# Selective-scan kernel: tiles of 4 states by 32 channels in place of one state by 128 channels

## What is computed

```
proj = x @ W_in.T;  hs, gate = split(proj);  hs = silu(causal_conv4(hs) + conv_b)
dt_r, Bm, Cm = split(hs @ W_x.T);  dt = softplus(dt_r @ W_dt.T + b_dt);  A = -exp(A_log)
state = exp(dt * A) * state + dt * B_t * u_t        # [128 channels, 16 states], per step
y = sum over states of state * C_t;  y = (y + hs * Dp) * silu(gate);  out = y @ W_out.T
```

## Time and profile before

| | us |
|---|---|
| median of 3 runs (lowest, highest) | 967.57 (965.07, 967.77) |
| profiled execution | 965.7 |
| its span | 963.9 |

### The profile page before, as it was taken

The page is one execution under the profiler, slowest core; times in us unless marked ns, Lnnn a source line. Parts: engine busy times, 40 slices in busy tenths (PEclk is TensorE's granted clock), DMA queues, the critical chain, the costliest instruction groups (busy, mean ns, idle before and its releaser), DMA issues.

```text
span 963.9 us, 8874 instructions
## 1 busy us (share of the span) xinstructions
PE 846.2 (88%) x2178; PEld 363.3 (38%) x2178; DVE 839.9 (87%) x632; ACT 585.7 (61%) x798; POOL 819.0 (85%) x374
## 2 busy tenths in 40 slices
PE   5688989989898899989989898998989889898776
PEld 2233433334443334334343333333443333433322
DVE  2489999888999988998998999999899989889991
ACT  3575765848476583855758486574857657484331
POOL 0598997979989797997989799898989979798990
PEclk9799999989999998989999999999999999899997
DMA  1699688978778798778869788896988779689760
GB/s 46 222 295 305 244 274 285 315 261 281 262 291 303 260 313 293 260 252 288 314 255 318 266 282 258 306 312 253 309 283 280 262 285 325 244 301 302 263 247 3
DMA packets 78051, 258.35 MB, mean 268 GB/s; under 512 B 13104, under 2 KB 15408, under 8 KB 78000
## 3 DMA queue, kind: packets, MB, share of 16 engines
q1 hardware_dynamic: 78000, 257.79, 77.4%
HBM read 254.60 MB, written 3.15 MB: 267 GB/s over the span
## 4 chain that ended last, share of the span: by engine, by line
POOL 51%; DMA 17%; issue 17%; PE 6%; DVE 5%; ACT 3%; SPq 1%; POOLq 1%; DVEq 0%; ACTq 0%
POOL inp L881 31%; POOL state L887 17%; DMA b_all<-bc_dram 14%; DMA c_all<-bc_dram 3%; POOL du L871 3%; DVE ps_x L1031 2%; PE ps_y L546 1%; DVE state L1031 1%; PE ps_w L459 1%; DVE state L1038 1%; ACT ps_x L730 1%; PE ps_x L531 1%; SPq L308 0%; PE ps_w L507 0%; POOL step L873 0%
## 5 line engine op out<-in xcount | busy, mean ns | idle before, releaser
L881 POOL TENSOR_TENSOR inp<-du,b_all 128x1024 f32<-128x1024 f32 x224 | 521.9, 2354 | 4.9 <-DMA b_all<-bc_dram 4.0
L546 PE MATMUL ps_y<-state,packed 128*128 128x512 f32 x1024 | 495.6, 623 | 19.5 <-POOL state L887 19.5
L1031 DVE TENSOR_TENSOR_SCAN ps_x<-ps_x,inp 128x1024 f32<-128x1024 f32 x144 | 329.3, 2287 | 42.5 <-ACT ps_x L730 29.8
L887 POOL TENSOR_TENSOR state<-state,c_all 128x1024 f32<-128x1024 f32 x112 | 262.0, 2351 | 87.0 <-DVE state L1024 49.4
L730 ACT ACTIVATE ps_x<-step,a_neg 128x1024 f32<-128x1024 f32 x224 | 247.1, 1112 | 137.7 <-DVE state L1038 101.0
L546 PEld LDWEIGHTS ps_y<-state,packed 128*128 128x128 f32 x1024 | 194.2, 197 | 267.5 <-issue 213.0
L1038 DVE TENSOR_TENSOR state<-ps_x,c_all 128x1024 f32<-128x1024 f32 x144 | 175.9, 1222 | 4.2 <-issue 0.7
L1031 DVE TENSOR_TENSOR_SCAN state<-ps_x,inp 128x1024 f32<-128x1024 f32 x80 | 179.1, 2272 | 0.0
L531 PE MATMUL ps_x<-u,w_b_wide 128*128 128x512 f32 x128 | 68.0, 656 | 9.4 <-DVE state L1038 9.3
L1024 DVE TENSOR_TENSOR_SCAN state<-decay,ps_x 128x1024 f32<-128x1024 f32 x32 | 73.0, 2281 | 0.5
L459 PE MATMUL ps_w<-xpad,w_conv 128*128 128x512 f32 x128 | 61.6, 605 | 3.3 <-ACT xpad L692 3.3
(11 more groups left out here) (116 smaller groups left out, 676.4 us busy)
## 6 DMA issues: line engine op xcount, KB each, us to landing
c_all<-bc_dram SPq DMA_DIRECT2D x256, 512.0 KB, 6.8
b_all<-bc_dram SPq DMA_DIRECT2D x224, 512.0 KB, 6.0
xt<-in_x_t SPq DMA_DIRECT2D x32, 64.0 KB, 3.3
bc_dram<-bc_rows SPq DMA_DIRECT2D x32, 64.0 KB, 3.2
out<-ofin SPq DMA_DIRECT2D x16, 64.0 KB, 1.6
packed<-in_packed SPq DMA_DIRECT2D x1, 635.0 KB, 4.2
packed<-in_packed SPq DMA_DIRECT2D x1, 129.0 KB, 2.1
w_qkv<-in_w_qkv SPq DMA_DIRECT2D x1, 64.0 KB, 2.2
```

The source lines that it names most:

```text
L546: last = mm(ps_y[:, HALF * half:HALF * (half + 1)], ident, state[n % H_RING][:, HALF * half:HALF * (half + 1)], start=(n == 0), stop=(n == ...
L881: tt(inp[i % IN_RING][:, :], du[b.buf][:, :], b_all[i % B_RING][:, :], ALU.mult).then_inc(pool_inputs, 1)
L887: tt(state[n % H_RING][:, :], state[n % H_RING][:, :], c_all[n % C_RING][:, :], ALU.mult).then_inc(pool_products, 1)
L1031: v.tensor_tensor_scan(held if KIND[n] == "P" else x, x, inp[i % IN_RING][:, :], 0.0, ALU.mult, ALU.add).then_inc(scans, 1)
```

## The change

A tile is now 4 states by 32 channels: tile n = 4m + q holds states 4m to 4m+3 (quad m) of channels 32q to 32q+31 (group q); partition 4i + k is channel i, state k. There are still 16 tiles of [128, 1024] per image, with the same four pieces of work.

- B and C: one load carries the four rows of a quad, repeated 32 times, and serves its 4 tiles: 4 loads of B and 4 of C per image in place of 14 and 16. Rings of 3.
- step and du have one value per channel; each of the 4 groups needs its 32 rows repeated 4 times. SP makes these `step_q` and `du_q` by DMA from SBUF to SBUF (`copy_step`, `copy_du`), 4 and 4 per image, in rings of 6. step and du themselves have one buffer instead of two, so `softplus` and `scan_weight` of the next image wait for the copies of the image before. `copy_step` needs also the first elements of each sequence set to a large step (`stops_set`), which POOL does after du.
- Sums: `sum_quad` replaces `sum_state`. A quad's 4 tiles are summed over the states into the 4 groups of 32 rows of `ps_y`, by matmuls with a stationary tile of 32 columns; it waits for the products of all four tiles.
- KIND has 3 D, 5 P and 8 C in place of 2 D, 5 P and 9 C.
- The softmax's normalisation moves from DVE to ACT: 1 / sum as exp(-ln(sum)), and two scaled copies.
- `mean_square` of the image after next follows its `attn_out`, and all orders are written anew. `prologue` and `finish` are fitted to them.

```diff
-H_RING, C_RING, IN_RING, B_RING, D_RING, X2_RING = 8, 4, 4, 4, 4, 3
+H_RING, C_RING, IN_RING, B_RING, D_RING, X2_RING = 8, 3, 4, 3, 2, 3
+STEP_RING, DU_RING = 6, 6
...
+QUAD, GROUPS = 4, 4
+ROWS = I // GROUPS
...
-KIND = "DCCPDCCCCPPCPPCC"
+KIND = "DPPCCCDCPPCDCCPC"
...
+            def copy_step(j, q):
+
+                o = GROUPS * j.num + q
+                sp.wait_ge(stops_set, j.num + 1)
+                if o >= STEP_RING:
+                    before = o - STEP_RING
+                    all_at_least(sp, *decays_waits(before // GROUPS, tiles_of_group(before % GROUPS)))
+                sp.dma_start(step_q[o % STEP_RING][:, :],
+                             step[ROWS * q:ROWS * (q + 1), :].unsqueeze(1).broadcast_to([ROWS, QUAD, T])
+                             ).then_inc(step_copied[o % STEP_RING], 16)
...
+            def copy_du(j, q):
...
+                sp.dma_start(du_q[o % DU_RING][:, :],
+                             du[ROWS * q:ROWS * (q + 1), :].unsqueeze(1).broadcast_to([ROWS, QUAD, T])
...
+            def load_b(b, m):
...
+                             bc_dram[b.buf][QUAD * m:QUAD * (m + 1), :].unsqueeze(0).broadcast_to([ROWS, QUAD, T])
...
+            def load_c(b, m):
...
+                sp.dma_start(c_all[o % C_RING][:, :],
+                             bc_dram[b.buf][N + QUAD * m:N + QUAD * (m + 1), :].unsqueeze(0
+                                            ).broadcast_to([ROWS, QUAD, T])).then_inc(c_loaded[o % C_RING], 16)
...
+            def sum_quad(b, m):
+
+                all_at_least(pe, *products_waits(b.num, tiles_of_quad(m)))
+                if m == 0:
...
                 for half in range(2):
-                    last = mm(ps_y[:, HALF * half:HALF * (half + 1)], ident,
-                              state[n % H_RING][:, HALF * half:HALF * (half + 1)],
-                              start=(n == 0), stop=(n == N - 1))
+                    for q in range(GROUPS):
+                        last = mm(ps_y[ROWS * q:ROWS * (q + 1), HALF * half:HALF * (half + 1)], w("sum_w"),
+                                  state[(GROUPS * m + q) % H_RING][:, HALF * half:HALF * (half + 1)],
+                                  start=(m == 0), stop=(m == QUAD - 1))
                 last.then_inc(sums, 1)
...
+            def attn_norm(j):
+                act.wait_ge(esc_done, j.num + 1)
+                f(lsum[:, :], esum[:, :], ACT.Ln).then_inc(lsum_done, 1)
+                act.wait_ge(lsum_done, j.num + 1)
+                f(erec[:, :], lsum[:, :], ACT.Exp, scale=-1.0).then_inc(erec_done, 1)
+                act.wait_ge(erec_done, j.num + 1)
+                at_least(act, attn_t_ps, j.num)
+                for k in range(CHUNKS):
+                    last = f(attn[:, k, :], attn_bank(j)[:, POOLED * k:POOLED * (k + 1)], ACT.Copy,
+                             scale=erec[:, k:k + 1])
+                last.then_inc(attn_done, 1)
...
-                at_least(act, du_done, j.num - 1)
-                f(step[j.buf][:, :], ps_w[:, :], ACT.Softplus, bias=w("b_dt")).then_inc(step_done, 1)
+                if j.num > 0:
+                    for q in range(GROUPS):
+                        o = GROUPS * (j.num - 1) + q
+                        act.wait_ge(step_copied[o % STEP_RING], 16 * (o // STEP_RING + 1))
+                f(step[:, :], ps_w[:, :], ACT.Softplus, bias=w("b_dt")).then_inc(step_done, 1)
```

More of the change, by code:

```diff
@@ new lines, in load_b @@
+            def load_b(b, m):
+                if m not in LOADED:
+                    return
+                o = NLB * b.num + LOADED.index(m)
+                sp.wait_ge(bc_stored, 32 * (b.num + 1))
+                if o >= B_RING:
+                    before = o - B_RING
+                    all_at_least(sp, *[(s, v) for s, v in inputs_waits(
+                        before // NLB, tiles_of_quad(LOADED[before % NLB])) if s is pool_inputs])
+                sp.dma_start(b_all[o % B_RING][:, :],
+                             bc_dram[b.buf][QUAD * m:QUAD * (m + 1), :].unsqueeze(0).broadcast_to([ROWS, QUAD, T])
+                             ).then_inc(b_loaded[o % B_RING], 16)
@@ L338, in prologue @@
                 load_x(first + 1)
+                copy_step(first, 0)
                 store_bc(first)
+                copy_du(first, 0)
+                copy_step(first, 1)
+                copy_step(first, 2)
+                copy_du(first, 1)
+                load_b(first, 0)
+                copy_du(first, 2)
+                load_c(first, 0)
                 load_b(first, 1)
+                copy_du(first, 3)
+                copy_step(first, 3)
                 load_b(first, 2)
-                load_b(first, 3)
-                load_b(first, 5)
-                load_c(first, 0)
                 load_c(first, 1)
-                load_c(first, 2)
-                load_b(first, 6)
-                load_c(first, 3)
             def finish(j):
@@ L638, in steps @@
                     attn_out(later)
+                    mean_square(later)
+                sum_quad(b, 3)
             program(pe, prologue, steps, finish)
@@ L780, in prologue @@
                 softmax_exp(first)
+                attn_norm(first)
                 state_decay()
@@ L1066, in prologue @@
                 attn_setup()
-                attn_norm(first)
                 conv_setup()
@@ L1083, in steps @@
                 scan(b, 0)
-                scan(b, 1)
+                if coming:
+                    rms(coming)
                 if done:
                     gated(done)
-                if coming:
-                    rms(coming)
-                product(b, 1)
+                scan(b, 1)
                 scan(b, 2)
-                product(b, 2)
                 scan(b, 3)
@@ L1103, in steps @@
                 scan(b, 8)
[L1104 removed]
                 scan(b, 9)
                 scan(b, 10)
+                if later:
+                    pooling(later)
+                scan_input(b, 11)
+                product(b, 10)
                 scan(b, 11)
+                scan(b, 12)
+                if later:
+                    row_max(later)
+                scan(b, 13)
+                product(b, 12)
                 if done:
                     out_norm(done)
[L1110 to L1117 removed]
+                product(b, 13)
                 scan(b, 14)
[L1119 removed]
                 scan(b, 15)
```

298 lines of the change are left out of this document (146 added, 152 removed).

## The result

The changed kernel takes 1026.6 us (median of 4 runs, 1016.8 to 1033.1) where the kernel before takes 966.3 on the same chip: a ratio of 1.061 [1.058, 1.065]. It is 6% slower; the ratio leaves out the one run of 1033.1 us, which fell in a slower state of the chip. The forecast was 930 us, 4% faster.

The account below looks back on a forecast made before the run. DVE's floor of 51.6 us per image plus waits of 0.2, 0.9, 1.2 and 0.3 gave 54.2 for 56.63; with start +4.5 and end -5, span 927, plus 1.8 and 1.2: 930 us, range 898 to 960.

Parts of the forecast that it names:

- the DMA term: Bunched copies and loads behind decay 12: third transfer lands after 8 us, just in time for POOL's input 1, costing nothing.
- L: Time from issue of copy_step 2 until load_b 0 lands; taken as 8 us, bounds 6 to 18.
- The rival with 8%: Copies bound the round from gated, 43.3 + L; decides from L = 10.9, slower from 13.3; 980 us at 14; chance 8%.
- DVE and POOL: Work per image on these two engines after the change: DVE 51.6 us, POOL 51.1 us.
- Which waits make it up: Waits added to DVE's 51.6 us per image: 0.2 decay 9, 0.9 spread 11, 1.2 closing, 0.3 conv 1 and spread 6.
- the closing term: PE from attn_turn at the low clock through spread 0 to sum_quad 3 ends at 49.5, not 48.3: 1.2 us per image.
- Quad sums: The eight matmuls of a sum_quad on PE run together in 2.1 us, bounds 2.1 to 7.5.
- PE's work: PE's work per image falls from 51 us to about 31.
- DMA share: Share of the time the DMA engines are busy: about 0.45 after the change, from 0.82.
- PE's clock: Two falls per image after idling, before bc_proj and before attn_turn; mean granted clock 0.7 to 0.85 of full.
- POOL's hole: POOL's 4.47 us wait per image ahead of product 0, to be filled by inputs 3 and 4.
- The start: First image waits for copies before its first B: scan 1 at about 47, +4.5 us, bounds +2 to +8.

Follow-up runs that it names:

- spread-source kernel: Changed kernel with channels regrouped (group q holds channels 4i + q), so each SBUF copy reads every fourth partition, not 32 neighbours: 943.5 us, 0.979 of the kernel before.

## Why the prediction was wrong, step by step

**The step that failed** is the DMA term: "I take 8, nearer to the loads, since a copy moves the same 128 rows of 4 KB". It looked at what a copy writes and not at what it reads. Decay 12 of the image shown ended at 514.1, and POOL had B rows at 525.7: L = 11.7 (mean of 15 images 12.0), inside the bounds of 6 to 18, but above the 10.9 from which the prediction let the copies be the bound. In the spread-source kernel decay 12 ended at 523.5 and POOL had B at 531.1: 7.6. The 8 that I took is what the bunch costs when its copies read partitions spread over all 128.

**The rival with 8% came true**: "the copies are the new bound". Its chance was 8%, and its arithmetic was not right either: its sum gives 43.3 + 11.7 = 55.0, which is still faster than the 56.6 before; the round of that image took 58.7, from gated at 477.8 to gated at 536.5. The 3.7 that it lacked are two of its other terms: 36.2 up to the end of decay 12 in place of 33.9 (1.45 of it DVE's wait for spread 11 and 0.5 its wait for decay 9), and 3.64 for the last sums in place of 2.1. The first is no matter of the copies: the spread-source kernel has the same 36.2. The second is: PE stood idle for 2.00 us until POOL had product 14, and ran at the low clock, where with the spread source it had no gap and ran at the full one.

The same round of the spread-source kernel took 54.6 (gated at 487.26 and 541.88). So the slow copies cost this image 4.1 us: L is 4.0 longer; 1.6 of that falls into a time in which the last sums would have stood behind mean_square on PE anyway (they start 1.8 us after POOL's product 14 there, 0.15 here); and the sums themselves are 1.7 longer at the low clock. The mean image took 59.6 for 54.6; why some images take longer than others I have not traced.

The Trainium skill ("SBUF — State Buffer", Door 1) spoke for this rival, and the rates of the runs agree with it: it says that 32 neighbouring partitions reach only half of the ports by which DMA gets at SBUF, and by its table of partition bits every fourth partition reaches all. Measured were 225 to 248 GB/s for the one, 398 to 419 for the other. The runs show rates; the ports themselves are in no trace. The estimate of L of about 9 that I drew from it was short of the 11.7. It counted three transfers alone; SP's rows suggest why (the stores of B and C, copy_du 0 and both step copies are in flight as well), but I have not measured their shares. By that estimate too the time would have been unchanged, so the Trainium skill made the rival likelier and did not give the loss.

**The other steps.** *DVE and POOL:* right. Work per image was 51.6 and 51.3 for the forecast 51.6 and 51.1, and with quick copies the image takes 54.6 for the forecast of 54.2. *Which waits make it up:* partly wrong. In the spread-source kernel DVE waits 2.1 us per image for spreads (forecast 0.9, and 0.9 more inside the closing term), 0.5 for decay 9 (0.2), 0.4 for the other decays (none), and hardly ever for the sums (3.3 us in all; forecast 1.2 per image). 51.6 + 2.1 + 0.5 + 0.4 is the 54.6. That the forecast came so near is in part luck: errors of both signs. *Quad sums:* right, 1.93 for 2.1, at the full clock. *PE's work:* too low, 40.9 us per image for about 31, at a mean granted clock of 0.78. *DMA share:* 0.59 for about 0.45, and 0.44 with the spread source. *PE's clock:* the two falls are where forecast, and in the changed kernel a third comes before the last sums. PE's timeline of the changed kernel: it idles 4.37 us before bc_proj (forecast 5) and 4.13 before attn_turn (forecast 6.9), spread 11 takes 3.69 (3.5); all that is much the same in the spread-source kernel (4.38, 4.43, 3.69).:

```profile
501.90 1.92 PE L561 MATMUL ps_w<-u,packed 128*32 128x512 f32 x4 [4.37 <-ACT step L793]
...
506.77 3.69 PE L610 MATMUL ps_x<-u,w_b_wide 128*128 128x512 f32 x4
...
519.47 1.12 PE L508 MATMUL ps_w<-packed,attn 128*64 128x128 f32 x4 [4.13 <-ACT attn L737]
```

*POOL's hole:* the prediction had it filled. It is gone ahead of product 0 and came back ahead of input 1; with quick copies it is at most 1.2 us there from 200 to 900.

**The start** was missed by 11 us: scan 1 at 57.98 for "about 47". DVE's timeline:

```profile
44.04 1.23 DVE L1092 TENSOR_TENSOR ps_x<-du_q,ps_x 128x1024 f32<-128x1024 f32 x1 [14.55 <-DMA du_q<-du]
...
56.88 0.42 DVE L1085 TENSOR_TENSOR xn<-x,ps_w 128x256 f32<-128x256 f32 x1 [6.93 <-ACT ps_w L760]
```

I had counted the copies up to input 1 on POOL. But DVE's own first input waits for copy_du 0, until 44.04 (38.03 with the spread source), and pooling, nmax and the whole attention of the second image stand behind that input in DVE's order and ahead of scan 1: 13.9 us more. The spread source still starts 9.6 us later than the kernel before (51.98 for 42.40). *The end* was right, 4.2 us shorter for 5.

In terms of the sum (of the span): 927 forecast, + 11 of start, + 15 x 5.8 of image, + 1 of end = 1026; 1025.6 measured. On the way from the span to 930 the prediction added 1.2 where its own figure was 1.9; that is 0.7 us and changes nothing.

## What to carry to other kernels

Cost a copy within SBUF by the partitions that it reads as well as by those that it writes; where the layout is free, give each group every n-th partition and not a block. When transfers fall in bytes but stand in one bunch behind one wait, work out the round that goes through that wait, and give the case in which it decides the weight that its bounds give it (here 6 to 18 us with the threshold at 10.9, which is not 8%). A part that moves between engines is worth what its place in the order makes it.

## What the runs showed of the hardware

- A copy of step of 512 KB that reads 32 neighbouring partitions lands after 8.1 us (median), one that reads 32 partitions spread over 128 after 4.4, one that reads HBM after 5.4, all in this kernel's queue. Copy_step 0 of one image, with the DMA engines idle ahead of it: 6.6, 3.5 and 3.7.
- From 100 to 900 us, issuing one load of B or copy of du held SP for up to 3.9 us in the changed kernel (median 2.1) and for at most 1.3 with the spread source (medians 0.8 and 0.6): a slow copy delays what follows it in SP's order twice.
- Matmuls with a matrix of zeros raise the granted clock (0.84 to 0.91, 0.78 to 0.92), though every product in them is zero.
- The matmuls of a quad, four column tiles of 32 side by side, ran in 1.93 us where 128 columns took 7.13, a factor of 3.7.
